# Handing the rows of C to the channels: four one-partition DMAs per state in place of one four-partition DMA

## The reference

```
dA = exp(d_t[..., None] * A)
h = dA * h + (d_t * u_t)[..., None] * b_t[:, None, :]
y_t = jnp.einsum('bdn,bn->bd', h, c_t)
```

## Time and profile before

| | |
|---|---|
| time, median of 3 runs | 427.69 us |
| the 3 runs | 427.69, 424.73, 428.63 us |
| the profiled execution | 426.04 us |
| its span (first to last instruction) | 424.3 us |
| mean granted TensorE clock | 0.977 |
| PE, DVE, ACT, POOL busy | 368.8, 306.4, 286.9, 166.5 us |
| state stage (first Cs DMA issued to last product ended) | 136.3 to 282.8 us |
| wait of POOL's product L542 for a Cs DMA | 16.4 us, 6 times |

### The profile page before, as it was taken

The page is one execution under the profiler, slowest core; times in us unless marked ns, Lnnn a source line. Parts: engine busy times, 40 slices in busy tenths (PEclk is TensorE's granted clock), DMA queues, the critical chain, the costliest instruction groups (busy, mean ns, idle before and its releaser), DMA issues.

```text
span 424.3 us, 11081 instructions
## 1 busy us (share of the span) xinstructions
PE 368.8 (87%) x4065; PEld 254.5 (60%) x4065; DVE 306.4 (72%) x631; ACT 286.9 (68%) x600; POOL 166.5 (39%) x142
## 2 busy tenths in 40 slices
PE   5799999999999597989499775998978989999996
PEld 4577777777755243444154342453954579888885
DVE  2869887698664989888269889985758957555554
ACT  3588899999967868759646793359974364444443
POOL 8314132232201438833985899970722400000000
PEclk9969999999999999999979999999999989999998
DMA  7120000002314272462222222200020001111111
GB/s 160 9 21 8 2 3 1 0 0 56 76 28 108 106 175 101 129 160 98 102 103 102 103 80 102 105 12 0 14 65 2 2 1 23 19 20 22 21 22 27
DMA packets 28496, 23.23 MB, mean 55 GB/s; under 512 B 20928, under 2 KB 22720, under 8 KB 28464
## 3 DMA queue, kind: packets, MB, share of 16 engines
q1 hardware_dynamic: 28068, 22.77, 19.8%
q10 hardware_dynamic: 396, 0.05, 0.1%
HBM read 2.00 MB, written 1.61 MB: 9 GB/s over the span
## 4 chain that ended last, share of the span: by engine, by line
PE 38%; DVE 24%; issue 16%; ACT 9%; POOL 8%; DMA 3%; SPq 1%; DVEq 1%; ACTq 1%; POOLq 0%
PE pair L1683 6%; DVE pair L1976 3%; PE pair L1174 3%; POOL hC L542 3%; PE pair L1185 3%; PE pair L1134 3%; DVE stats L1757 3%; PE pair L1299 2%; DVE Ts L1867 2%; PE pair L1193 2%; PE pair L1671 2%; DMA vec<-in_L_conv_b_qkv 2%; PE pair L1156 2%; PE pair L1352 2%; PE pair L1228 2%
## 5 line engine op out<-in xcount | busy, mean ns | idle before, releaser
L542 POOL TENSOR_TENSOR hC<-Hs,Cs 128x784 f32<-128x784 f32 x31 | 59.6, 1929 | 38.4 <-DVE Hs L1988 17.3
L510 POOL TENSOR_TENSOR Km<-Ks,mask 128x784 f32<-128x784 f32 x16 | 24.1, 1508 | 71.0 <-ACT Ks L717 71.0
L1352 PE MATMUL pair<-hC,ident 128*128 128x392 f32 x128 | 48.6, 504 | 1.3 <-POOL hC L542 1.2
L1861 DVE TENSOR_REDUCE mx<-pair 128x8 f32<-128x392 f32 x64 | 33.0, 556 | 19.3 <-PE pair L1134 19.2
L1976 DVE TENSOR_TENSOR pair<-DU,pair 128x392 f32<-128x392 f32 x64 | 35.6, 556 | 15.3 <-PE pair L1348 15.1
L1683 PE MATMUL pair<-hst,BD 128*128 128x112 f32 x224 | 37.7, 299 | 2.1 <-DVE Rt L2241 0.4
L1174 PE MATMUL pair<-ident,Pr 113*113 113x113 f32 x256 | 37.3, 280 | 2.5 <-issue 1.6
L1174 PEld LDWEIGHTS pair<-ident,Pr 113*113 113x113 f32 x256 | 31.2, 184 | 12.8 <-issue 12.0
L1348 PE MATMUL pair<-BCf,sel 96*128 96x392 bf16 x64 | 21.8, 343 | 16.6 <-DVE Hs L1988 9.7
L1988 DVE TENSOR_TENSOR_SCAN Hs<-dA,Hs,pair 128x392 f32<-128x392 f32 x32 | 33.0, 1030 | 3.6
L1683 PEld LDWEIGHTS pair<-hst,BD 128*128 128x128 f32 x224 | 30.0, 195 | 9.1 <-DVE hst L2235 5.2
(11 more groups left out here) (254 smaller groups left out, 840.8 us busy)
## 6 DMA issues: line engine op xcount, KB each, us to landing
Cs<-BCf SPq DMA_DIRECT2D x32, 392.0 KB
SX<-XP SPq DMA_DIRECT2D x16, 336.8 KB, 5.9
XT<-in_x SPq DMA_DIRECT2D x4, 392.0 KB, 7.0
out<-Os SPq DMA_DIRECT2D x28, 56.0 KB, 1.7
AD<-Aa SPq DMA_DIRECT2D x4, 196.0 KB
NB<-in_L_conv_x_proj_w SPq DMA_DIRECT2D x4, 3.0 KB
DW<-in_L_conv_dw SPq DMA_DIRECT2D x4, 1.1 KB
W<-in_L_conv_w_qkv ACTq DMA_DIRECT2D x1, 48.0 KB
```

What stands on the lines that cost most here:

```text
L542: eng.tensor_tensor(hC[:, i % NHC, :], Hs[:, i % NHS, :], Cs[i % NCS][:, :], ALU.mult).then_inc(v_c, 1)
L1352: return eng.matmul(STATES[:, h, :], ident[:, :], src[:, columns(h)], start=first, stop=last)
L1861: eng.tensor_reduce(mx[:, g, :], banks[g][:, 0:392].rearrange("p (m k) -> p m k", k=WT), AX.X, ALU.max).then_inc(max_r, 1)
```

## The change

For each turn, the one DMA over four source partitions (stride 8) becomes a loop over the four images. Each DMA of the loop reads one partition of BCf, 3,136 bytes, 32 times over, and writes it to the 32 partitions of its image. All four raise the same semaphore by 16 each, so whoever waits for the buffer waits for 64 where it waited for 16. Waits ahead of the DMA stay where they were, before the first of the four. Two lines are added, so line numbers above 440 grow by two.

```diff
-                    eng.dma_start(Cs[i % NCS][:, :], bcast(BCf[3 * C + n:P:DS, c % 2, :], 1, C)).then_inc(s_cs[i % NCS], 16)
+                    for g in range(G):
+                        row = 3 * C + DS * g + n
+                        eng.dma_start(Cs[i % NCS][C * g:C * g + C, :], bcast(BCf[row:row + 1, c % 2, :], 1, C)).then_inc(s_cs[i % NCS], 16)
...
-                    eng.wait_ge(s_cs[i % NCS], 16 * (i // NCS + 1))
+                    eng.wait_ge(s_cs[i % NCS], 16 * G * (i // NCS + 1))
...
-                    eng.wait_ge(s_cs[(DS * J - 1) % NCS], 16 * (DS * J // NCS))
+                    eng.wait_ge(s_cs[(DS * J - 1) % NCS], 16 * G * (DS * J // NCS))
...
-            eng.wait_ge(s_cs[i % NCS], 16 * (DS * J // NCS))
+            eng.wait_ge(s_cs[i % NCS], 16 * G * (DS * J // NCS))
```

## The result

The changed kernel takes 469.81 us (467.19 to 470.02, 4 runs) against 427.61 us before: ratio 1.0985, 95% interval 1.0919 to 1.105. The profiled execution has a span of 468.0 us, 43.7 us more than before. It is slower, as forecast, by 42 us where 76 us were forecast.

The account below looks back on a forecast made before the run. Cs transfers, with shifted copies, were taken to fill the state stage. Span 424.3 + 76.2 us for slower transfers = 500.5, 502.3 with 1.74 around it, plus 1.65 for the runs' median: 504 us; own range 455 to 620 us.

Parts of the forecast that it names:

- What bounds the kernel: State stage: Cs transfers and shifted copies fill 140.7 of 146.5 us; longer transfers lengthen it, shorter ones gain little.
- How many engines: Cs DMAs in the state stage: all 16 DMA engines at work on each, where four worked before.
- The door at the side that is read: Cs reads: neighbouring partitions share one door of 25.3 GB/s, whoever reads; a turn through one door costs 15.9 us.
- The engines drift apart: Cs DMAs of a turn: engines done early read the next image's partition by another door; four doors give 3.97 us.
- I take the middle of one and four doors, 2.5: Cs transfers: 63.2 GB/s, 6.35 us a turn, 203.2 us for 32 against 127.0, so +76.2 us.
- The issues: SP's queue: 96 more DMAs at 547 ns, 52.5 us, hidden under the 6.35 us turn and SP's 77 us waiting.
- by issues alone: Rival on SP's queue: four issues a turn at 1.2 us each, +27 us, about 454 us without any door; chance 0.05.
- What the profile would show: State stage of the changed kernel: predicted length, DMA share and rate, POOL's Cs waits over 60 us, first turn's landing.
- The faster rival: State stage: reading one partition is no limit, a turn's transfer at most 2.0 us, DVE late next, about 420 us; chance 0.13.

Follow-up runs that it names:

- The two kernels with fast transfers: Cs DMAs read many partitions of XN instead of BCf: four DMAs a turn against the changed kernel, 417.56 us; one against the kernel before, 418.39 us.
- the two-pair kernel: Against the kernel before, each turn's DMA cut into two, each of two images and so two source partitions: 548.08 us.
- neighbouring partitions: Against the changed kernel, image g's rows read from partition 96 + g of BCf in every turn (wrong rows): 769.2 us.
- half rows: Against the changed kernel, each Cs DMA cut into two of half a row, 256 DMAs in all with the same bytes: 532.33 us.
- two queues: Against the changed kernel, images 2 and 3 issued on ACT's queue after each dA, images 0 and 1 on SP's as before: 453.39 us.
- many doors: Against the changed kernel, each of the 128 Cs DMAs reads 32 different partitions of XN instead of one of BCf: 417.56 us.
- Partitions 32 apart: Against the changed kernel, image g read from partition 32g of XN in every turn (other data than C): 602.3 us.
- one DMA at a time: Against the changed kernel, SP waits after each Cs DMA until it has landed: 960.27 us.

## Why the prediction was right, and where its size was off

*What bounds the kernel.* Right. The transfers filled the stage before, and 45.1 us more of stage are the whole difference. The two kernels with fast transfers show the other half of the statement, that shorter ones gain little: 8 us, and DVE is late next.

*How many engines.* Right: the share went from 0.26 to 0.94, and the two-pair kernel shows the cut by source partitions by itself.

*The door at the side that is read.* Right, and shown by changing only what is read: 470 against 418 us, 769 with neighbouring partitions. One door carries 27 GB/s with 16 engines on it, a little over the 25.3 of one engine.

*The engines drift apart.* The direction was right; a turn takes 5.28 us, between the 3.97 of four doors and the 14.9 of one. The landing events of the changed kernel show the drift itself: the first landing of a turn comes 1.1 us (median) before the last one of the turn before, and 9 (median) of that turn's 64 landings come after it; with neighbouring partitions it is none. At 1.3 us an image, the leading engine is by estimate one to two images ahead of the last, not turns.

*The step that was off* is "I take the middle of one and four doors, 2.5". It was a choice between two ends and not worked out, so that the range of 455 to 620 us holds the result says little about this step. Measured are 3.0: 5.28 us a turn and not 6.35, 32 x 1.07 = 34 us less, which is the difference between the forecast and the measurement. (By the rate the turns account for 32 x 1.31 = 42 of the 45.1 us of stage; I have not placed the other 3.) The reason I gave for a low number, that a leader may be four turns ahead at most and POOL then frees no buffer, was not at work: SP waited for a buffer 1.7 us in all. The reading that fits in its place is that some four DMAs are in flight from one queue, and part of each one's life isn't transfer. The runs with half rows and with two queues speak for that; they don't say where the limit sits, and with 4.7 in flight for half rows it isn't exactly a count. That bunching within a DMA adds to it isn't ruled out.

*The issues.* I hid them at 547 ns under the turn. They lie at 1,284 ns, but as a symptom: 592 ns with many doors. The rival "by issues alone" foretold 454 us by a wrong mechanism, and its row, issues of over 1 us in bursts, was itself backlog in all likelihood.

*What the profile would show.* Stage about 220 us: it is 191.6. POOL's wait over 60 us: 74.3. Share near 1.00 at 50 to 75 GB/s: 0.94 at 76. The landing of the first turn 16 us after its issue: wrong, the last of its landing events is 9.6 us after it, at 145.6 us, which fits first DMAs that are read through several doors. (POOL's first product starts at 145.9 us, and the profile names DVE's Hs as what it waited for.) *The faster rival* was sized right (420 us; 418 where its condition holds), and it doesn't hold here.

## What to carry to other kernels

Count the DMA engines from the share in a window (0.25 is four of 16) and the rate of each; before putting more engines on a transfer, ask through how many doors they will read at a time, for 16 engines on one partition are hardly faster than one (27 to 29 GB/s against 25.3). Here partitions 96 to 99 were one door, 8 apart were different doors, and 0, 32, 64 and 96 made fewer than four. A DMA queue whose issues become long, with a chain of waits that runs through it, may only be showing the backlog of its transfers: change what is read and leave the issues alone to find out. A row that has to be handed to many partitions may be better read from copies in DRAM, with an outermost dimension of 16; here that gained 8 us over four partitions read by four engines.

## What the hardware showed that I had not expected

- About four DMAs are in flight from one queue (4.1 to 4.7 over four kernels whose landing times go from 4.5 to 15.0 us); cutting the same bytes into twice as many DMAs raised the time from 470 to 532 us.
- Partitions 32 apart share the door for reads (602 us with two doors), while two engines that write 32 apart are not slowed: in the kernel before each keeps 25.3 GB/s. In the two-pair kernel the packets of its two engines start 5 to 43 ns apart and last 124 to 132 ns, so both write at once; that they are 32 apart at that moment takes for granted that each goes through its rows in order.
- Where PE waits longer for the transfers, its mean granted clock is lower: 0.977 before, 0.954 in the changed kernel, 0.761 with neighbouring partitions and 0.714 with one DMA at a time. In the last two whole slices stand at 0.5, the lower level of 1.2 GHz. POOL waits there for 381 and 562 us in all for Cs DMAs, so I take it that the clock isn't where their time goes; no run separates the two.
